# Four attention and feed-forward layers on one core: part of the next attention's opening moved into the last block of the second and third feed-forward stage

## What is computed

```
x = x + L0_xattn(layernorm(x), ctx); x = x + L0_ffn(layernorm(x))      # quantised ffn
x = x + L1_xattn(layernorm(x), ctx); x = x + L1_ffn(layernorm(x))      # 8 experts, top 2, + a shared one
x = x + L2_xattn(layernorm(x), ctx, mask); x = x + L2_ffn(layernorm(x))  # layernorm, causal attention, layernorm, 8 gated experts
x = x + L3_xattn(ctx, ctx, layernorm(x), mask); x = x + L3_ffn(layernorm(x))
```

## Time and profile before

| what | value |
|---|---|
| median of 3 runs | 1942.22 us (1940.82 to 1944.78) |
| the profiled execution's own time | 1943.53 us |
| its span, first to last instruction | 1941.7 us |
| PE busy | 1749.6 us, 90% |
| DVE busy | 1149.1 us, 59% |
| ACT busy | 1084.7 us, 56% |
| POOL busy | 589.3 us, 30% |
| DMA moved | 132.38 MB |

### The profile page before, as it was taken

One profiled execution on the slowest core, in us unless ns is written; L12 is line 12 of the kernel. 1 busy time (PEld: TensorE's weight loads), 2 busy tenths in 40 slices (PEclk: granted clock), 3 DMA queues, 4 the chain that ended last, 5 costly groups with the idle time before them and its releaser, 6 DMA issues.

```text
span 1941.7 us, 38864 instructions
## 1 busy us (share of the span) xinstructions
PE 1749.6 (90%) x14438; PEld 1188.5 (61%) x14476; DVE 1149.1 (59%) x3394; ACT 1084.7 (56%) x2172; POOL 589.3 (30%) x1171
## 2 busy tenths in 40 slices
PE   5999955899979999979999999979996999989997
PEld 2555524455548889944444455558883555569997
DVE  5788846688852332236777656636664888633443
ACT  1788831488864444426677755533332888844442
POOL 5344212233312221122333344323324344122221
PEclk9999977699999999969999999979995999989999
DMA  4443200455300000023323134300004454100000
GB/s 142 128 126 121 76 16 14 128 169 175 104 18 1 1 1 1 1 87 113 102 92 99 40 115 134 92 1 1 1 1 129 146 155 137 35 1 7 6 7 6
DMA packets 114854, 132.38 MB, mean 68 GB/s; under 512 B 14934, under 2 KB 78700, under 8 KB 114668
## 3 DMA queue, kind: packets, MB, share of 16 engines
q1 hardware_dynamic: 114668, 129.90, 22.1%
HBM read 83.45 MB, written 46.40 MB: 67 GB/s over the span
## 4 chain that ended last, share of the span: by engine, by line
PE 76%; issue 7%; DVE 7%; ACT 6%; POOL 1%; DMA 1%; SPq 0%; POOLq 0%; DVEq 0%
PE ps_s L1303 14%; PE ps_av L1078 13%; PE ps_s L1036 12%; PE ps_t L1281 9%; PE ps_t L1051 4%; PE ps_s L1281 3%; ACT prob L845 3%; PE ps_t L1062 3%; DVE mx L1435 3%; PE ps_m L1086 2%; PE ps_m L1134 2%; PE ps_m L1120 2%; PE ps_m L1126 2%; PE ps_m L1113 2%; PE ps_t L1064 1%
## 5 line engine op out<-in xcount | busy, mean ns | idle before, releaser
L845 ACT ACTIVATE prob<-ps_t 128x512 f32<-128x512 f32 (+1 forms) x1152 | 616.5, 586 | 169.8 <-PE ps_t L1051 161.7
L1435 DVE TENSOR_REDUCE mx<-ps_s 128x1 f32<-128x512 f32 x768 | 487.3, 683 | 110.9 <-PE ps_s L1036 109.4
L1036 PE MATMUL ps_s<-kst,qst 32*128 32x512 f32 (+2 forms) x1280 | 387.1, 490 | 43.3 <-DVE mx L1435 22.4
L1303 PEld LDWEIGHTS ps_s<-w_ffn,prob 128*128 128x128 f32 x2688 | 314.2, 192 | 8.3
L1303 PE MATMUL ps_s<-w_ffn,prob 128*128 128x128 f32 x2688 | 318.4, 276 | 0.0
L1036 PEld LDWEIGHTS ps_s<-kst,qst 32*128 32x128 f32 x1280 | 166.7, 192 | 241.4 <-issue 98.1
L1051 PE MATMUL ps_t<-qmx,kst 32*128 32x256 f32 (+1 forms) x2304 | 306.4, 334 | 6.1 <-ACT prob L845 6.1
L1078 PE MATMUL ps_av<-prob,vaug 128*32 128x256 f32 (+1 forms) x4608 | 307.2, 386 | 2.7 <-ACT avs L886 2.7
L985 ACT ACTIVATE prob<-ps_t,b1c 128x512 f32<-128x512 f32 x204 | 125.3, 685 | 240.9 <-PE ps_t L1281 240.9
L1669 DVE SCALAR_TENSOR_TENSOR avs<-ps_s,comb,avs 128x128 f32<-128x128 f32 x336 | 94.6, 344 | 260.4 <-PE ps_s L1303 260.4
L785 POOL TENSOR_TENSOR kst<-w_ffn,kst 128x512 fp32r<-128x512 f32 x100 | 127.1, 1273 | 371.3 <-ACT kst L970 371.3
(11 more groups left out here) (209 smaller groups left out, 2151.3 us busy)
## 6 DMA issues: line engine op xcount, KB each, us to landing
kst<-k_parts SPq DMA_DIRECT2D x128, 256.0 KB, 3.4
qst<-q_parts SPq DMA_DIRECT2D x160, 128.0 KB, 3.6
k_parts<-k_hi SPq DMA_DIRECT2D x64, 256.0 KB, 3.0
q_parts<-q_hi SPq DMA_DIRECT2D x80, 128.0 KB, 2.4
ctxT<-in_ctxT SPq DMA_DIRECT2D x32, 256.0 KB, 2.7
k_parts<-k_lo SPq DMA_DIRECT2D x32, 256.0 KB, 3.5
q_parts<-q_lo SPq DMA_DIRECT2D x40, 128.0 KB, 2.4
w_ffn<-in_F_w SPq DMA_DIRECT2D x18, 256.0 KB, 3.3
```

The lines of the kernel that those rows point to most:

```text
L845: nc.scalar.activation(row[:, S * kt:S * kt + w], ps_t[TURN[unit(ph, g, n) % 8]][:, 0:w], ACT.Exp).then_inc(sig["exp_done"], 1)
L1036: pe.matmul(dst, qst[p][strip, g, q * 128:(q + 1) * 128], kst[p][strip, g, 0:nk], start=True, stop=True).then_inc(sig["s_ready"], 1)
L1303: mm = pe.matmul(dst, h[:, c, 128 * q:128 * (q + 1)], w2c, start=(c == 0 and not bias), stop=(c == nc_h - 1))
L1435: dve.tensor_reduce(mx[:, buf, i:i + 1], src, AX.X, ALU.max, negate=True).then_inc(sig["max_done"], 1)
```

## The change

A table `LEADS` gives, for the last block of F1 and of F2, what is issued for the next attention's batch 0 at which place: `(e, "mid")` is between `first_product(e+1)` and `second_product(e)`, `(e, "end")` behind `second_product(e)`. The numbers 0 to 5 are pairs of plain score products, that is the first 12 of the 16 of groups 0 and 1. The remaining two pairs stay in `attention`. The scores of this opening go to `ps_av` and `ps_m` in place of the three `ps_s`, which the experts use. Nothing of the arithmetic is changed. A0, A1, AS and F3 keep their order.

```
+LEADS = {
+    "F1": {(0, "end"): "K", (1, "end"): "XT", (2, "end"): "Q", (3, "end"): "V", (4, "mid"): "B0", (4, "end"): "B1",
+           (5, "end"): 0, (6, "mid"): 1, (6, "end"): 2, (7, "mid"): 3, (7, "end"): 4, (8, "end"): 5},
+    "F2": {(0, "end"): "K", (1, "end"): "XT", (2, "end"): "Q", (3, "end"): "V", (4, "mid"): "B0",
+           (4, "end"): 0, (5, "mid"): 1, (5, "end"): 2, (6, "mid"): 3, (6, "end"): 4, (7, "end"): 5},
+}
+LED = {"A2": "F1", "A3": "F2"}
+LED_PAIRS = 6
...
-        x_hi, x_lo = k_hi, k_lo
-        w_parts = [(kst[p][:, n, :], kst[p][:, n + 1, :]) for p, n in ((1, 0), (1, 2), (0, 0))]
+        x_hi = sb("x_hi", [128, SK], F32R)
+        x_lo = sb("x_lo", [128, SK], F32R)
+        w_third = sb("w_third", [128, 2, SK], F32R)
...
-        combT = kf[0:E + 1, :]
+        combT = sb("combT", [E + 1, SK])
...  POOL, normalise_batch: block 0's statistics are enough for batches 0 and 1
+                elif ph in LED:
+                    wait(pool, "rstd_done", cnt.at("rstd_done", LED[ph], bt.b // 2))
...  POOL, start of the attention
+                if ph in LED:
+                    split_maxima(ph, b0, 0)
+                    normalise_batch(ph, b1)
                     if ph == "A3":
-                        prepare_masks(b0)
+                        prepare_masks(b1)
+                    split_maxima(ph, b0, 1)
...  POOL, experts, last block
+                    if last and ph in LEADS:
+                        lead("XT")                      # masks of batch 0 (A3), then normalise_batch
                     for e in range(turn, ne if last else ne + turn):
                         low_weights(blk + e // ne, e % ne)
+                        if last and ph in LEADS:
+                            lead({turn + 1: "K", turn + 3: "Q"}.get(e))
...  ACT, experts, last block, behind expert e
+                        if last and ph in LEADS and e:
+                            lead(e - 1)                 # the copy out of ps_m of K, XT, Q or V
...  PE, scores
+                if led(ph, bt, g):
+                    bank = (ps_av, ps_m)[i % 2]
+                    wait(pe, "max_done", cnt.at("max_done", ph, bt, 8 * g + i) - 2)
+                    if i % 2:
+                        take_misc("max_done", cnt.at("max_done", ph, bt, 8 * g + i))
...  PE, start of the attention
+                if ph in LED:
+                    for pair in range(LED_PAIRS, 8):
+                        lead(ph, pair)
+                    wait(pe, "acc_done", cnt.start("acc_done", ph))
+                    wait(pe, "h_done", cnt.start("h_done", ph))
+                    wait(pe, "g_done", cnt.start("g_done", ph))
+                    maxima_T(ph, b0, 0)
...  PE, experts
+                        if last and ph in LEADS:
+                            lead({"F1": "A2", "F2": "A3"}[ph], LEADS[ph].get((e, "mid")))
                         second_product(blk, e, e)
+                        if last and ph in LEADS:
+                            lead({"F1": "A2", "F2": "A3"}[ph], LEADS[ph].get((e, "end")))
...  DVE, experts (maxima or the bias copy), and start of the attention
+                        if last and ph in LEADS:
+                            lead({"F1": "A2", "F2": "A3"}[ph], LEADS[ph].get((e, "mid")))
                         accumulate(blk, e)
+                        if last and ph in LEADS:
+                            lead({"F1": "A2", "F2": "A3"}[ph], LEADS[ph].get((e, "end")))
```

More of the change, by code:

```diff
@@ L344, in unit, with led @@
             return HG * pairs(ph) * g + n
+        def led(ph, bt, g):
+            return ph in LED and bt.b == 0 and g < 2
         def unit_at(ph, k, half):
@@ L890, in maxima_T, with widen_bias @@
                 nc.scalar.activation(qmx[:, g % 2, :], ps_m[:, 0:S], ACT.Copy).then_inc(sig["mt_read"], 1)
+            def widen_bias(ph):
+                if ph in BIASED:
+                    wait(act, "bias_in", cnt.start("bias_in", ph))
+                    nc.scalar.activation(bv_wide[:, :], ident[:, :], ACT.Identity, bias=b_att[ph][:, 2:3], scale=0.0).then_inc(bv_widened, 1)
             def attention(ph):
                 b0 = Batch(0)
[L894 to L897, removed]
+                if ph in LED:
+                    maxima_T(ph, b0, 0)
+                elif ph != "AS":
+                    widen_bias(ph)
                     for what in ("K", "XT", "Q", "V"):
@@ L970, in high_weights, with lead @@
                     nc.scalar.activation(halves(w_parts[e % turn][0]), first_weights(ph, e), ACT.Copy).then_inc(sig["wh_done"], 1)
+                def lead(e):
+                    ph_next = {"F1": "A2", "F2": "A3"}[ph]
+                    for part in ("mid", "end"):
+                        what = LEADS[ph].get((e, part))
+                        if what == "K":
+                            widen_bias(ph_next)
+                        if what in ("K", "XT", "Q", "V"):
+                            misc(what, ph_next, Batch(0))
                 def body(blk, last):
@@ L1033, in scores @@
                     nk = 128 * (q + 1)
-                wait(pe, "max_done", cnt.at("max_done", ph, bt, 8 * g + i) - BACK[i])
-                dst = ps_s[TURN[i]][:, 0:nk]
+                if led(ph, bt, g):
[3 more added lines that the diff above has]
+                        take_misc("max_done", cnt.at("max_done", ph, bt, 8 * g + i))
+                else:
+                    bank = ps_s[TURN[i]]
+                    wait(pe, "max_done", cnt.at("max_done", ph, bt, 8 * g + i) - BACK[i])
+                dst = bank[:, 0:nk]
                 pe.matmul(dst, qst[p][strip, g, q * 128:(q + 1) * 128], kst[p][strip, g, 0:nk],
@@ L1148, in misc, with lead @@
                     mm.then_inc(sig["o_ready"], 1)
-            def attention(ph):
-                if ph != "AS":
+            def lead(ph, what):
+                b0 = Batch(0)
+                if what == "K":
+                    misc_reader[0] = None
+                    if ph == "A2":
+                        for a in watt_in:
+                            pe.wait_ge(watt_in[a], 64)
+                    if ph == "A3":
+                        pe.wait_ge(bd_loaded, 16 * 3 * H)
+                if what in ("K", "XT", "Q", "V"):
+                    misc(what, ph, b0)
+                elif what in ("B0", "B1"):
+                    output_bias(ph if what == "B0" else "AS")
+                elif what is not None:
+                    if what == 0:
+                        wait(pe, "lg_read", cnt.start("lg_read", ph))
+                        wait(pe, "ct_read", cnt.start("ct_read", ph))
+                    for i in (2 * what, 2 * what + 1):
+                        scores(ph, b0, i // 8, i % 8)
+            def attention(ph):
+                b0 = Batch(0)
+                if ph in LED:
+                    for pair in range(LED_PAIRS, 8):
[3 more added lines that the diff above has]
+                    wait(pe, "g_done", cnt.start("g_done", ph))
+                    maxima_T(ph, b0, 0)
+                elif ph != "AS":
                     wait(pe, "acc_done", cnt.start("acc_done", ph))
@@ L1155, in attention @@
                     misc_reader[0] = None
[L1156 to L1163, removed]
+                    for what in ("K", "XT", "Q", "V"):
+                        misc(what, ph, b0)
+                    output_bias(ph)
                 if ph == "A0":
@@ L1169, in attention @@
                     mm.then_inc(w1_across, 1)
-                for g in range(0 if ph == "AS" else 2):
+                for g in range(0 if ph == "AS" or ph in LED else 2):
                     for i in range(8):
@@ L1340, in _ @@
             for ph in PHASES:
-                if ph == "A3":
-                    pe.wait_ge(bd_loaded, 16 * 3 * H)
                 if ph in ATT:
@@ L1432, in maximum @@
                     nk = 128 * (q + 1)
-                src = ps_s[TURN[i]][:, 0:nk]
+                src = ((ps_av, ps_m)[i % 2] if led(ph, bt, g) else ps_s[TURN[i]])[:, 0:nk]
                 if mask in (None, "keys"):
@@ L1490, in convert_rest, with lead @@
                 link(dve.tensor_scalar(mask_T[:, :, :], mask_T_i, 0.0, MASKED, ALU.is_equal, ALU.mult))
+            def lead(ph, what):
+                if what in ("B0", "B1"):
+                    output_bias(ph if what == "B0" else "AS")
+                elif isinstance(what, int):
+                    for i in (2 * what, 2 * what + 1):
+                        maximum(ph, Batch(0), i // 8, i % 8)
             def attention(ph):
                 b0 = Batch(0)
-                if ph != "AS":
+                if ph in LED:
+                    for pair in range(LED_PAIRS, 8):
+                        lead(ph, pair)
+                elif ph != "AS":
                     wait(dve, "x_new", cnt.start("x_new", ph))
@@ L1498, in attention @@
                     quantise_weights()
[L1499 to L1503, removed]
+                if ph != "AS" and ph not in LED:
+                    output_bias(ph)
+                    for g in range(2):
```

(2 more changed lines are left out.)

15 lines of the change are left out of this document (12 added, 3 removed).

## The result

| | before | after |
|---|---|---|
| median of the runs | 1943.5 us (4 runs, 1940.8 to 1945.8) | 1920.6 us (4 runs, 1919.5 to 1923.7) |
| the profiled execution's span | 1941.7 us | 1917.7 us |
| its mean granted clock | 0.941 | 0.952 |

The ratio is 0.9868, with a 95% interval of 0.9824 to 0.9911: 1.3% faster. The median fell by 22.9 us and the span by 24.0, where 28.4 was forecast; 1920.6 lies inside the range and 6.6 us above the predicted time. Single executions of one kernel here lie 10 to 20 us apart when a longer part of one runs at the lower clock, so wherever a few us matter I compare the lengths of stages in the traces, and not only medians.

A forecast was written before the change was run, and what follows sets the result against it. PE, busy 90%, was taken as the bound, with time won where it idles or runs slowly. Tails 19.1 + 21.7 less 12.4 in the blocks gives 28.4 us off the 1942.2 median: 1914, range 1903 to 1924.

The forecast's parts named there:

- The tails: From the last `second_product` to the first `scores_T`: 9.1 us in A2, 9.5 in A3, DVE setting the pace.
- The blocks: Last blocks of F1 and F2: moved work and stalls lengthen them, 6.0 and 6.4 us, 12.4 together.
- the two readings of the durations: Moved work in the last blocks: upper ends 6.8 and 6.0 us, overlapped 5.4 and 5.0; middle 6.0 and 5.5.
- The waits in F2: F2's last block: an iteration's second pair finds its odd bank late, some 0.4 us, twice, 0.9 us.
- POOL's mask conversion: A3's conversion, 1.93 us, now ahead of `low_weights(2)` in F2; costs up to 1.9 us once if slack is gone.
- Separate buffers cost nothing: Giving the moved work its own buffers was costed at zero us.
- The loop's half-clock stretch stays as it is: Start of the A2 and A3 loops: the clock still falls in the tail; stretches stay 15.9 and 15.7 us.
- rival 1: Clock stays up or comes back earlier at the openings: 5 to 14 us more gain, about 1905; chance 0.12.
- rival 2: Strips or DVE stop PE inside the blocks: 5 to 9 us go, about 1921; chance 0.12.
- rival 3: Clock falls inside the blocks from pair 0 on: 15 us slower, 1957; chance 0.03.

The follow-up runs named there:

- maxima first: The changed kernel with the last four maxima and their scores ahead of `result`, and POOL's split ahead of `power`: 1919.3 us, ratio 0.9863 to the kernel before.
- near: The changed kernel with `x_hi`, `x_lo` and `w_third` laid right behind `k_lo`: 1919.4 us, ratio 0.9881 to the kernel before; repeated, 1912.2 us.
- preparation only: The changed kernel without moved scores, all 16 plain scores behind the last block: 1933.6 us, ratio 0.9947 to the kernel before.

## Why the prediction was right

The direction and the mechanism were right, and the time was 6.6 us above the forecast: inside the whole range, but 0.6 above the 1909 to 1920 that the forecast gave itself without the rivals. Step by step:

**The tails** came out as built up: 8.8 and 9.6 us against 9.1 and 9.5. DVE did set the pace, in the order forecast, with each of PE's last products released by a maximum. The experiment with the maxima first confirms it: taking `result` and the statistics out of the chain took 2.3 to 2.8 us off, the size of that term.

**The blocks** grew by 6.8 and 7.3 us against 6.0 and 6.4. About 0.5 us of each is the slower pace (8 or 9 `first_product` at 62 ns), which leaves 6.3 and 6.7 for the moved work; the middle I took between the two readings of the durations was right within 0.3. In F1 that is a little luck: the pairs cost 0.54 us each where I had 0.43, so the rest cost less than I took. The waits in F2 were where I put them, at 0.33 us twice against 0.9 in all. POOL's mask conversion cost little of the 1.9 us that I had as its upper end: it ran at 1409.15, and behind it the weight load of `first_product(2)` waited 0.72 us for POOL's low part, until 1414.12. From the start of K to that product it took 0.91 us, against 0.46 at the same place in F1, so the delay was at most 0.5 us.

**"Separate buffers cost nothing"** is the step that failed. It was written without any row. In stage lengths it cost 1.5 us in F3, about 1 in the last blocks and up to 1.1 in the other blocks, 3 to 4 us; near gives back 2.9 of it. The rows I had couldn't show it, because before only one placement of these operands existed; I should have carried it as an unknown with a bound on each side.

**"The loop's half-clock stretch stays as it is"** was half right. The clock fell where it was said to, 3.7 us behind T; in A3 it stayed down until 14.6 us into the loop, in A2 only until 8.5, which is rival 1 in a small form. That gave 2.5 of the 2.7 us in A2 and AS (the 33rd transposed product starts 19.6 us into the loop, against 22.1 before). In A3's loop 2.2 us went the other way: 6.8 us at 0.50 from 1668.3, ahead of the 13.7 us that end the phase in both kernels. The kernel with A2 alone, whose A3 is untouched, has it too (228.7 us), and near, whose A3 is the changed one, doesn't (226.8), so it isn't of the moved work.

**The rivals.** Strips and DVE didn't stop PE in the blocks (rival 2): pair 0 waited for no DMA. The clock didn't fall in the blocks that got the 32-row products (rival 3): both block windows above have 1.00. The Trainium skill's "TensorE: Matmul & The Clock Gate", section "A second HAM failure mode: psum-queue depth-cycling", would have it go to and fro there; those rows don't agree. The stretches at the start of F2's blocks, behind a short wait of PE, come nearer to it, but at 10 of 39 places, and none of them in the rows of this kernel. Rival 2's time of 1921 was hit by accident and for another reason, which is why the time alone would not have told the causes apart.

The missing 4.4 us of the span are thus: placement 3.6, the moved work itself 0.6, the front part 0.8, less 0.1 in the tails and 0.5 in the loops. The front, before F1, is not touched by the change, and its 0.8 us are within what such executions differ by.

## What to carry to other kernels

When a phase opens with a chain of latencies and the phase before ends on a full engine, issue that chain from inside the full phase: it costs what the moved products cost there at full clock (here 13 us for two openings) and gives back what of the chain no longer stands behind the phase (41 of 59 us). Price a new buffer by its place too: keep the operand that a product streams as near to the one it loads as weights as it was, and compare the distance between the starts of equal products before and after. Once an opening is short, look at the clock's row behind it, since what an idle engine loses there can be more than the idle time that is left.

## What the runs showed of the hardware

- The distance between starts of dense 128x128 by 512-column products was 227 ns with tokens and weights 2,000 to 33,000 bytes apart (from start to start of the buffers) in the lower part of a partition, and 233 ns with 131,000 bytes and more between them, all at a granted clock of 1.00. I hadn't expected any dependence. With both at the top, 2,000 to 22,500 bytes apart, it was about 2 ns more than near ((2612 - 2591) / 11). That small remainder isn't shown to come from the place: with the weights in `w_third`, at the same addresses as in the changed kernel, the sum is 2611 ns there, 2597 when it was run again and 2591 in the kernel with preparation only.
- A stretch at half clock around an opening lasted 41.0 and 44.4 us before, 13.7 and 20.5 after, and 0 and 3.4 with PE kept busy. Over the whole span the lower clock was granted for 231 us before and 185 after.
- Ten stretches of 3.4 us at 0.50 stood in F2 in five of thirteen traces, PE busy throughout, each 2.8 to 3.6 us behind the start of a block's gate products, where PE had been idle for some 1 us; at 29 more such places the clock held. Another of 44.4 us stood inside the loop of AS, with PE busy for 43.95 us of it; in the 9.8 us before it PE had been idle for 1.1. Why the clock fell in these executions and not in the others stays open.
